# A routed expert kernel: the last expert's low parts on VectorE, each gather one job sooner

## The chip, the cores and the metric

The kernel runs on one core of a Trainium2 chip. The metric is the device time of one launch in microseconds. The core has TensorE (PE: matmuls and transposes), VectorE (DVE), ScalarE (ACT), GpSimd (POOL) and a queue on SyncE (SP) that only issues transfers. Each engine works through its own instructions in order; between engines there are only semaphores.

## The reference

For 4 x 512 tokens of 512 features, attention without values comes first, and then a mixture of experts:

```python
x = x + softmax(scores(ctx @ Wq.T + bq, ctx @ Wk.T + bk) * layernorm(x) + mask)   # (4, 512, 512)
t = layernorm(x)                                    # 2048 tokens x 512
shared = silu(t @ shared_gate_w) * (t @ shared_up_w) @ shared_down_w
logits = t @ router_w                               # 8 experts, the best 2 are taken
probs  = sigmoid(logits) at the two best, 0 elsewhere
gate, up = split(einsum('etd,edf->etf', probs.T[:, :, None] * t, gate_up_w))
out = x + shared + einsum('eti,eid->etd', silu(gate) * up, down_w).sum(axis=0)
```

## The kernel before

Work is cut into 55 jobs of 128 rows. Jobs 0 to 15 are the 16 tiles of tokens; each passes through the attention and then the shared expert, at place 0 of the weights. Jobs 16 to 54 are the 39 routed jobs: each has 128 rows of one expert. In between (about 121 to 145 us) DVE works out from the logits which token goes into which row of which job, and writes the tables jexpert (expert of a job), jgather and jscatter (rows to fetch and to add to), and jneed (see below). Experts follow one another in order, so that those of a low number come first; the trace shows four or five jobs for each.

Every product in the mixture is made of three: high by high, high by low and low by high. A tensor is split into a rounded high part and a low part, the difference of value and high part. For the weights this is done once. They come in 27 chunks (CHUNKS) of 128 x 1024 values, three to each expert: c // 3 is the place and c % 3 the third, two for gate_up and one for down. The SP queue loads a chunk into one of three stage buffers (L276), ScalarE makes the high part (high_part, L501, semaphore hi_s) and GpSimd the low part (low_part, L362, semaphore lo_s). SP's load of chunk c waits until chunk c-3 has its low part. Most chunks are done under the shared jobs. Chunks 22 to 24 get their low parts (late_low) after the first four gathers and 25 and 26 between the routed jobs, where ScalarE makes their high parts after jobs 17 and 18. The last chunks' places were used by other buffers until then (the four xn rows, for one), hence the waits in late_low.

A routed job n has these steps. GpSimd gathers its rows from the normalized tokens in memory into xg (gather, L423), four buffers deep. TensorE transposes them (x_transpose, L1133) while it works on job n-1; ScalarE makes x_hi and x_bf (L514, L515), DVE x_lo (L679). TensorE then makes the gate and up products (L963, L968, L1007), ScalarE the activation (L603), DVE the gating product h (gated, L878, semaphore h_s), the last to read xg. TensorE transposes h (L1016), its parts are made (L522, L523, and h_low at L685), and TensorE makes the down product (L1028, L1031, L1034) within job n+1. DVE copies it to y (y_routed, L887), four buffers deep, and GpSimd adds y to the output rows (scatter, L442) by an accumulating transfer.

In job n TensorE's order is: gate and up high of n, transpose of h of n-1, gate and up rest of n, transposes of n+1, down of n-1. DVE's order is: h_low(n-1), gated(n), x_low(n+1), y_routed(n-1).

Two rows of one token in jobs of different experts may not be added at the same time. So a scatter waits on GpSimd for the completion of the three scatters before it: always while n < 23 (named first in the code), and after that as jneed says, only where the expert differs. The buffers of y are given back by the same completions. All gathers and scatters stand in GpSimd's one queue, gather(n+4) and then scatter(n), as the loop at L458 to L463 writes them.

TensorE waits before each routed job for the low parts of its weights: for the first eight jobs up to the expert's own third chunk (jlow), after that for all of them.

Of the kernel before, what the change touches and what calls it, by code (L numbers as in the profile page):

```python
# [8 lines left out]
TILES = T // P  # L9
# [7 lines left out]
JOBS = TILES + ROUTED  # L17
# [6 lines left out]
XS = 4  # L24
# [7 lines left out]
NC = K * TILES  # L32
CAREFUL = 8
READY = EARLY + 1
FIRST = TILES - LAG
BIAS = 7


def build(nc, x, ctx, mask, kpad, wq, bq, wk, bk, router_w, gate_up_w, down_w, sg_w, su_w, sd_w, out):
# [10 lines left out]
    with stack:  # L50
        def sem(name):
            return stack.enter_context(nc.semaphore(name))
# [161 lines left out]
        st_trash, st_p8 = sem("st_trash"), sem("st_p8")  # L214

        c_ident, c_half, c_table, zero_s = sem("c_ident"), sem("c_half"), sem("c_table"), sem("zero_s")
        hi_s, lo_s, rwhi_s, rwlo_s = sem("hi_s"), sem("lo_s"), sem("rwhi_s"), sem("rwlo_s")
        bq_ready, wT_ps, wT_ready, ctxT_ps, ctxT_ready, proj_ps, proj_ready = (
            sem("bq_ready"), sem("wT_ps"), sem("wT_ready"), sem("ctxT_ps"), sem("ctxT_ready"), sem("proj_ps"),
            sem("proj_ready"))  # L220
# [88 lines left out]
        def _(pool):  # L309
# [63 lines left out]
                        zeros[:].unsqueeze(1).to_broadcast([P, XS, D])).then_inc(st_trash, 16)  # L373

            def late_low(c):
                place, i = c // 3, c % 3
                if i < 2:
                    t = TILES - XS + 2 * (place - 7) + i
                    pool.wait_ge(st_xn[t % XS], stored_xn(t))
                    pool.wait_ge(xT_ps, t + 1)  # L380
                else:
                    pool.wait_ge(max_s, TILES)
                low_part(c)
# [64 lines left out]
            pool.wait_ge(st_p8, 16)  # L448
            for n in range(TILES, TILES + XS):
                gather(n)  # L450
            for c in range(READY, READY + 3):
                late_low(c)
            for t in range(TILES - X2S, TILES):
                pool.wait_ge(st_y[t % X2S], stored_y(t))
            pool.wait_ge(st_trash, 16)
            pool.wait_ge(scatter_s, 1)
            pool.wait_ge(need_s, XS - 1)
            for n in range(TILES, JOBS):  # L458
                if n + XS < JOBS:
                    gather(n + XS)  # L460
                scatter(n)
                if n in (TILES + 1, TILES + 2):
                    late_low(READY + 3 + n - TILES - 1)  # L463
            for n in range(JOBS - XS, JOBS):
                pool.wait_ge(add_y[n % XS], 16 * ((n - TILES) // XS + 1))

# [154 lines left out]
        def _(dve):  # L621
# [74 lines left out]
            def y_shared(n):  # L696
                dve.wait_ge(y_ps, n + 1)
                dve.wait_ge(xn_s, n + 1)
                v.tensor_tensor(x2[:, n % X2S, :], ps_y(n)[:], x2[:, n % X2S, :], ALU.add).then_inc(y_s, 1)  # L699
# [136 lines left out]
            def tables():  # L836
# [4 lines left out]
                then(v.tensor_tensor(hole[:], hole[:], pidx[:, 0:ROUTED], ALU.mult))  # L841
                v.scalar_tensor_tensor(jscatter[:], tok[:], -1.0, hole[:], ALU.add, ALU.add).then_inc(scatter_s, 1)

            fetch(0, 0, FIRST)
            x_low(TILES - 2)
            last_normal()
# [21 lines left out]
            h_low(TILES - 2)  # L868
            scatter_waits()
            y_shared(FIRST - 1)  # L870
            h_low(TILES - 1)
            y_shared(TILES - 2)
            y_shared(TILES - 1)
# [16 lines left out]
            for n in range(TILES, JOBS):  # L890
                if n > TILES:
                    h_low(n - 1)
                gated(n)
                if n + 1 < JOBS:
                    x_low(n + 1)
                if n > TILES:
                    y_routed(n - 1)
# [4 lines left out]
        def _(pe):  # L902
# [236 lines left out]
            for n in range(TILES, JOBS):  # L1139
                e = pe.value_load(jexpert[0:1, n - TILES:n - TILES + 1], min_val=0, max_val=E)  # L1140
                if n < TILES + CAREFUL:
                    low = pe.value_load(jlow[0:1, n - TILES:n - TILES + 1], min_val=6, max_val=CHUNKS)
                    pe.wait_ge(lo_s, low)
                else:
                    pe.wait_ge(lo_s, CHUNKS)
                gate_up_high(n, e)
                if n > TILES:
                    h_transpose(n - 1)
                gate_up_low(n, e)
                gate_up_rest(n, e)  # L1150
                if n + 1 < JOBS:
                    x_transpose(n + 1)
                if n > TILES:
                    down(n - 1, before)
                before = e
# [24 lines left out]
```

## Time and profile before

| | us |
|---|---|
| median of 3 runs | 353.49 (353.42 to 355.19) |
| the profiled execution, its own time | 353.46 |
| its span, first to last instruction | 351.6 |
| TensorE busy | 318.0 (90%) |
| DVE busy | 206.8 (59%) |
| ScalarE busy | 181.0 (51%) |
| GpSimd busy | 212.2 (60%) |

The profile is of one execution. A span is counted from the first instruction to the last; the time of the execution has 1.86 us more around it. Job 16 begins on TensorE at 153.55 us and the last of its matmuls are at 343 us, so over half of the span is routed jobs.

### The profile page before, as it was taken

How to read it: one execution, taken by the hardware profiler on the slowest of the kernel's cores; microseconds unless marked ns; L12 is line 12 of the kernel's file. 1: busy time of each engine (PE TensorE's matmuls, PEld its weight loads, DVE VectorE, ACT ScalarE, POOL GpSimd, SP SyncE). 2: the span in 40 equal slices, each digit the busy share in tenths (PEclk: the TensorE clock that was granted, in tenths of full speed). 3: DMA queues.
4: the chain of work that ended last, by engine and by line, in shares of the span. 5: the costliest groups of instructions: out<-in, count | busy, mean ns of one | idle time of the engine just before them, and what ended most of it. 6: DMA issues, size and time to landing. Idle time of an engine off the chain costs nothing.

```text
span 351.6 us, 6597 instructions
## 1 busy us (share of the span) xinstructions
PE 318.0 (90%) x1677; PEld 222.4 (63%) x1677; DVE 206.8 (59%) x453; ACT 181.0 (51%) x409; POOL 212.2 (60%) x206
## 2 busy tenths in 40 slices
PE   2868999899999897879998989999999999999990
PEld 1334666676777666647766757777777777777760
DVE  0695888899998799834443444444444444445440
ACT  2578777767868745135544434444344444434430
POOL 0699999988686700393683666665465565555333
PEclk9989999999999999699999999999999999999998
DMA  7956678856755421281556486666666576565635
GB/s 175 320 216 230 213 239 241 245 204 209 236 159 187 170 92 7 66 292 38 90 97 115 70 170 99 109 110 118 117 122 108 88 128 108 115 123 100 113 45 75
DMA packets 29762, 50.60 MB, mean 144 GB/s; under 512 B 5472, under 2 KB 9312, under 8 KB 29728
## 3 DMA queue, kind: packets, MB, share of 16 engines
q0 software_dynamic: 9008, 21.66, 34.4%
q1 hardware_dynamic: 19232, 27.99, 24.7%
q10 hardware_dynamic: 1488, 0.54, 0.7%
q8 instruction: 16, 0.26, 0.3%
q14 instruction: 18, 0.15, 0.1%
HBM read 30.45 MB, written 19.73 MB: 143 GB/s over the span
## 4 chain that ended last, share of the span: by engine, by line
PE 60%; POOL 12%; DMA 10%; issue 9%; DVE 4%; SPq 2%; ACT 2%; POOLq 0%; DVEq 0%; ACTq 0%
PE bank L963 10%; PE bank L1007 10%; PE bank L968 8%; DMA out_rows<-y,jscatter 6%; PE bank L1028 4%; PE bank L1034 4%; PE bank L1031 4%; POOL gu_lo L362 4%; PE bank L1133 4%; PE bank L1016 2%; POOL dn_lo L362 2%; DMA xin<-in_x 2%; PE bank L926 2%; PE bank L985 2%; PE bank L935 2%
## 5 line engine op out<-in xcount | busy, mean ns | idle before, releaser
L442 POOL DMA_INDIRECT out_rows<-y,jscatter x39 | 61.9, 1587 | 74.1 <-DMA out_rows<-y,jscatter 52.1
L1007 PE MATMUL bank<-gu_hi,x_lo 128*128 (+1 forms) x220 | 72.8, 452 | 0.6 <-DVE x_lo L679 0.6
L963 PE MATMUL bank<-gu_hi,x_hi 128*128 (+1 forms) x220 | 61.6, 402 | 3.7 <-ACT x_hi L514 2.6
L423 POOL DMA_INDIRECT xg<-xn_rows,jgather x39 | 41.7, 1069 | 27.5 <-DVE jgather L839 15.3
L1007 PEld LDWEIGHTS bank<-gu_hi,x_lo 128*128 128x128 f32 x220 | 41.3, 189 | 18.0 <-issue 4.3
L878 DVE SCALAR_TENSOR_TENSOR h<-bank,xg,h 128x256 f32<-128x256 f32 x39 | 18.9, 484 | 56.0 <-ACT h L603 56.0
L522 ACT CAST h_hi<-bank 128x256 fp32r<-128x256 f32 x55 | 20.5, 374 | 60.7 <-PE bank L1016 57.0
L963 PEld LDWEIGHTS bank<-gu_hi,x_hi 128*128 128x128 f32 x220 | 40.0, 188 | 14.7 <-issue 2.8
L679 DVE TENSOR_TENSOR x_lo<-bank,x_hi 128x512 fp32r<-128x512 f32 x55 | 37.9, 690 | 19.0 <-ACT x_bf L515 18.6
L362 POOL TENSOR_TENSOR gu_lo<-stage,gu_hi 128x1024 bf16<-128x1024 f32 x18 | 43.4, 2410 | 5.6 <-ACT gu_hi L501 5.6
L603 ACT ACTIVATE h<-bank,xg 128x256 f32<-128x256 f32 x39 | 18.5, 474 | 50.0 <-PE bank L1007 26.4
L968 PE MATMUL bank<-gu_lo,x_bf 128*128 (+1 forms) x172 | 44.2, 379 | 0.0
L685 DVE TENSOR_TENSOR h_lo<-bank,h_hi 128x256 fp32r<-128x256 f32 x55 | 23.1, 420 | 32.9 <-ACT h_bf L523 32.8
L1034 PE MATMUL bank<-dn_hi,h_lo 128*128 (+1 forms) x86 | 35.5, 494 | 0.0
L514 ACT CAST x_hi<-bank 128x512 fp32r<-128x512 f32 x55 | 31.9, 581 | 6.3 <-PE bank L1133 4.3
L515 ACT CAST x_bf<-bank 128x512 bf16<-128x512 f32 x55 | 32.9, 598 | 0.0
L1028 PE MATMUL bank<-dn_hi,h_hi 128*128 (+1 forms) x86 | 30.8, 439 | 2.1 <-DVE x L699 1.0
L887 DVE COPY y<-bank 128x512 f32<-128x512 f32 x39 | 26.6, 681 | 1.3 <-PE bank L1034 1.3
L1031 PE MATMUL bank<-dn_lo,h_bf 128*128 (+1 forms) x86 | 26.5, 391 | 0.0
L1133 PE MATMUL bank<-ident,xg 128*128 128x128 f32 x156 | 23.5, 273 | 2.2 <-DMA xg<-xn_rows,jgather 2.2
L357 POOL TENSOR_TENSOR pen<-mask_pen,kpad_pen 128x512 bf16<-128x512 bf16 x16 | 18.6, 1160 | 10.1 <-DVE kpad_pen L705 10.0
L362 POOL TENSOR_TENSOR dn_lo<-stage,dn_hi 128x1024 bf16<-128x1024 f32 x9 | 21.9, 2438 | 4.5 <-ACT dn_hi L501 4.4
(145 smaller groups left out, 553.2 us busy)
## 6 DMA issues: line engine op xcount, KB each, us to landing
stage<-in_L_ffn_gate_up_w SPq DMA_DIRECT2D x16, 512.0 KB, 3.9
xin<-in_x SPq DMA_DIRECT2D x16, 256.0 KB, 4.4
xn_rows<-xn SPq DMA_DIRECT2D x16, 256.0 KB, 4.0
stage<-in_L_ffn_down_w SPq DMA_DIRECT2D x8, 512.0 KB, 3.7
out_rows<-x SPq DMA_DIRECT2D x16, 256.0 KB, 4.3
out_rows<-zeros POOLq DMA_DIRECT2D x1, 1024.0 KB, 5.0
ctx_in<-in_ctx SPq DMA_DIRECT2D x1, 768.0 KB, 8.8
xg<-xn_rows,jgather POOLq DMA_INDIRECT x39
```

Of the source, the lines that this page charges most:

```text
L362: g.tensor_tensor(third((gu_lo, dn_lo), c), stage[:, c % 3], third((gu_hi, dn_hi), c).bitcast(f32), ALU.subtract).then_inc(lo_s, 1)
L423: g.indirect_dma_start(out=xg[:, r, :], out_offset=None, in_=xn_dram, in_offset=bass.IndirectOffsetOnAxis(ap=jgather[:, n - TILES:n - TILE ...
L442: g.indirect_dma_start(out=out, out_offset=bass.IndirectOffsetOnAxis(ap=jscatter[:, n - TILES:n - TILES + 1], axis=0), in_=y[:, r, :], in_ ...
L515: a.copy(x_bf[:, n % TS], rows_T(n)).then_inc(xbf_s, 1)
L679: v.tensor_tensor(x_lo[:, n % TS], rows_T(n), x_hi[:, n % TS].bitcast(f32), ALU.subtract).then_inc(xlo_s, 1)
L963: tn.matmul(ps_g(n)[:], x_hi[:, n % TS, k, :], gu_hi[:, e, k, :], start=(k == 0), stop=False)
L968: tn.matmul(ps_g(n)[:], x_bf[:, n % TS, k, :], gu_lo[:, e, k, :], start=False, stop=False)
L1007: last = tn.matmul(ps_g(n)[:], x_lo[:, n % TS, k, :], gu_hi[:, e, k, :], start=False, stop=(k == KC - 1))
L1028: tn.matmul(ps_y(n)[:], h_hi[:, n % 2, c, :], dn_hi[:, e, c, :], start=(c == 0), stop=False)
L1031: tn.matmul(ps_y(n)[:], h_bf[:, n % 2, c, :], dn_lo[:, e, c, :], start=False, stop=False)
L1034: last = tn.matmul(ps_y(n)[:], h_lo[:, n % 2, c, :], dn_hi[:, e, c, :], start=False, stop=(c == IC - 1))
L1133: last = tn.transpose(ps_xT[n % 2][:, k * P:(k + 1) * P], xg[:, n % XS, k * P:(k + 1) * P], ident[:])
```

## The change

The low parts of chunks 24, 25 and 26 (the last expert, LAST = 24) are made by DVE instead of GpSimd, with a semaphore of their own, lolast_s. The first stands in DVE's order after the y of tile 13 and ahead of h_low(15); the other two in jobs 18 and 19 between h_low and the gating product. TensorE waits for lo_s up to 24 and, from job 24 on, for lolast_s too. GpSimd's loop issues gather(20) ahead of the loop and then gather(n+5) ahead of scatter(n), where it was gather(n+4). A gather's own wait (h_s of the job that held its buffer) is the same.

```diff
--- before.py
+++ after.py
@@ -32,6 +32,7 @@
 NC = K * TILES
 CAREFUL = 8
 READY = EARLY + 1
+LAST = CHUNKS - 3
 FIRST = TILES - LAG
 BIAS = 7
 
@@ -214,7 +215,7 @@
         st_trash, st_p8 = sem("st_trash"), sem("st_p8")
 
         c_ident, c_half, c_table, zero_s = sem("c_ident"), sem("c_half"), sem("c_table"), sem("zero_s")
-        hi_s, lo_s, rwhi_s, rwlo_s = sem("hi_s"), sem("lo_s"), sem("rwhi_s"), sem("rwlo_s")
+        hi_s, lo_s, lolast_s, rwhi_s, rwlo_s = sem("hi_s"), sem("lo_s"), sem("lolast_s"), sem("rwhi_s"), sem("rwlo_s")
         bq_ready, wT_ps, wT_ready, ctxT_ps, ctxT_ready, proj_ps, proj_ready = (
             sem("bq_ready"), sem("wT_ps"), sem("wT_ready"), sem("ctxT_ps"), sem("ctxT_ready"), sem("proj_ps"),
             sem("proj_ready"))
@@ -373,9 +374,8 @@
                         zeros[:].unsqueeze(1).to_broadcast([P, XS, D])).then_inc(st_trash, 16)
 
             def late_low(c):
-                place, i = c // 3, c % 3
-                if i < 2:
-                    t = TILES - XS + 2 * (place - 7) + i
+                if c % 3 < 2:
+                    t = TILES - XS + c % 3
                     pool.wait_ge(st_xn[t % XS], stored_xn(t))
                     pool.wait_ge(xT_ps, t + 1)
                 else:
@@ -448,19 +448,18 @@
             pool.wait_ge(st_p8, 16)
             for n in range(TILES, TILES + XS):
                 gather(n)
-            for c in range(READY, READY + 3):
+            for c in range(READY, LAST):
                 late_low(c)
             for t in range(TILES - X2S, TILES):
                 pool.wait_ge(st_y[t % X2S], stored_y(t))
             pool.wait_ge(st_trash, 16)
             pool.wait_ge(scatter_s, 1)
             pool.wait_ge(need_s, XS - 1)
+            gather(TILES + XS)
             for n in range(TILES, JOBS):
-                if n + XS < JOBS:
-                    gather(n + XS)
+                if n + XS + 1 < JOBS:
+                    gather(n + XS + 1)
                 scatter(n)
-                if n in (TILES + 1, TILES + 2):
-                    late_low(READY + 3 + n - TILES - 1)
             for n in range(JOBS - XS, JOBS):
                 pool.wait_ge(add_y[n % XS], 16 * ((n - TILES) // XS + 1))
 
@@ -841,6 +840,17 @@
                 then(v.tensor_tensor(hole[:], hole[:], pidx[:, 0:ROUTED], ALU.mult))
                 v.scalar_tensor_tensor(jscatter[:], tok[:], -1.0, hole[:], ALU.add, ALU.add).then_inc(scatter_s, 1)
 
+            def last_low(c):
+                if c % 3 < 2:
+                    t = TILES - 2 + c % 3
+                    dve.wait_ge(st_xn[t % XS], stored_xn(t))
+                    dve.wait_ge(xT_ps, t + 1)
+                else:
+                    dve.wait_ge(max_s, TILES)
+                dve.wait_ge(hi_s, c + 1)
+                v.tensor_tensor(third((gu_lo, dn_lo), c), stage[:, c % 3], third((gu_hi, dn_hi), c).bitcast(f32),
+                                ALU.subtract).then_inc(lolast_s, 1)
+
             fetch(0, 0, FIRST)
             x_low(TILES - 2)
             last_normal()
@@ -868,6 +878,7 @@
             h_low(TILES - 2)
             scatter_waits()
             y_shared(FIRST - 1)
+            last_low(LAST)
             h_low(TILES - 1)
             y_shared(TILES - 2)
             y_shared(TILES - 1)
@@ -890,6 +901,8 @@
             for n in range(TILES, JOBS):
                 if n > TILES:
                     h_low(n - 1)
+                if n in (TILES + 2, TILES + 3):
+                    last_low(LAST + n - TILES - 1)
                 gated(n)
                 if n + 1 < JOBS:
                     x_low(n + 1)
@@ -1139,10 +1152,11 @@
             for n in range(TILES, JOBS):
                 e = pe.value_load(jexpert[0:1, n - TILES:n - TILES + 1], min_val=0, max_val=E)
                 if n < TILES + CAREFUL:
-                    low = pe.value_load(jlow[0:1, n - TILES:n - TILES + 1], min_val=6, max_val=CHUNKS)
+                    low = pe.value_load(jlow[0:1, n - TILES:n - TILES + 1], min_val=6, max_val=LAST)
                     pe.wait_ge(lo_s, low)
                 else:
-                    pe.wait_ge(lo_s, CHUNKS)
+                    pe.wait_ge(lo_s, LAST)
+                    pe.wait_ge(lolast_s, CHUNKS - LAST)
                 gate_up_high(n, e)
                 if n > TILES:
                     h_transpose(n - 1)
```

## Rows read from the trace of the kernel before

**Rows 1.** Windows view: us, busy us (x instructions) of each engine, granted clock, DMA share, GB/s.

```profile
182.00:209.00 27.00, 24.68 (x123) 17.02 (x122) 11.24 (x21) 10.63 (x25) 15.94 (x12) 1.00 0.65 113
209.00:336.00 127.00, 127.00 (x644) 90.97 (x643) 58.47 (x108) 55.60 (x135) 69.59 (x52) 1.00 0.63 111
```

**Rows 2.** Timeline of TensorE: start us, us, engine, line, operation, idle before and its releaser.

```profile
157.86 1.19 PE L963 MATMUL bank<-gu_hi,x_hi 128*128 x4 [0.87 <-POOL gu_lo L362]
...
162.70 1.09 PE L963 MATMUL bank<-gu_hi,x_hi 128*128 x4
...
165.64 0.60 PE L1133 MATMUL bank<-ident,xg 128*128 128x128 f32 x4
...
168.38 0.38 PE L1016 MATMUL bank<-ident,h 128*128 128x128 f32 x2
...
181.70 1.09 PE L963 MATMUL bank<-gu_hi,x_hi 128*128 x4
...
185.65 0.66 PE L1133 MATMUL bank<-ident,xg 128*128 128x128 f32 x4 [0.85 <-DMA xg<-xn_rows,jgather]
...
187.85 1.20 PE L963 MATMUL bank<-gu_hi,x_hi 128*128 x4 [0.16 <-issue]
...
206.60 0.66 PE L1133 MATMUL bank<-ident,xg 128*128 128x128 f32 x4 [1.30 <-DMA xg<-xn_rows,jgather]
...
208.47 1.09 PE L963 MATMUL bank<-gu_hi,x_hi 128*128 x4
```

**Rows 3.** Chain that ended last, in order of time: start us, us, what.

```profile
164.82 4.86 DMA out_rows<-y,jscatter
...
201.07 5.49 DMA xg<-xn_rows,jgather
```

**Rows 4.** Timeline of GpSimd: low parts (L362), gathers (L423), scatters (L442).

```profile
146.71 1.03 POOL L423 DMA_INDIRECT xg<-xn_rows,jgather  x1 [0.30 <-issue]
...
150.41 2.39 POOL L362 TENSOR_TENSOR gu_lo<-stage,gu_hi 128x1024 bf16<-128x1024 f32 x1
...
155.08 2.36 POOL L362 TENSOR_TENSOR gu_lo<-stage,gu_hi 128x1024 bf16<-128x1024 f32 x1
158.68 1.03 POOL L423 DMA_INDIRECT xg<-xn_rows,jgather  x1 [1.24 <-DVE h L878]
164.82 1.64 POOL L442 DMA_INDIRECT out_rows<-y,jscatter  x1 [5.10 <-DVE y L887]
...
171.65 2.91 POOL L362 TENSOR_TENSOR gu_lo<-stage,gu_hi 128x1024 bf16<-128x1024 f32 x1
...
180.50 1.08 POOL L423 DMA_INDIRECT xg<-xn_rows,jgather  x1 [0.16 <-issue]
...
199.18 1.59 POOL L442 DMA_INDIRECT out_rows<-y,jscatter  x1 [2.69 <-DVE y L887]
201.07 1.07 POOL L423 DMA_INDIRECT xg<-xn_rows,jgather  x1 [0.30 <-issue]
```

**Rows 5.** Timeline of VectorE around the places of its new steps.

```profile
147.15 0.19 DVE L832 TENSOR_TENSOR other<-efl 128x38 f32<-128x38 f32 x1
...
150.78 0.42 DVE L685 TENSOR_TENSOR h_lo<-bank,h_hi 128x256 fp32r<-128x256 f32 x1 [1.90 <-ACT h_bf L523]
...
161.82 0.48 DVE L878 SCALAR_TENSOR_TENSOR h<-bank,xg,h 128x256 f32<-128x256 f32 x1 [1.42 <-ACT h L603]
...
166.55 0.49 DVE L878 SCALAR_TENSOR_TENSOR h<-bank,xg,h 128x256 f32<-128x256 f32 x1 [1.41 <-ACT h L603]
...
171.30 0.48 DVE L878 SCALAR_TENSOR_TENSOR h<-bank,xg,h 128x256 f32<-128x256 f32 x1 [1.40 <-ACT h L603]
```

**Rows 6.** Timeline of ScalarE: x_hi of job 17, high part of chunk 25.

```profile
157.07 0.58 ACT L514 CAST x_hi<-bank 128x512 fp32r<-128x512 f32 x1
...
162.50 1.08 ACT L501 CAST gu_hi<-stage 128x1024 fp32r<-128x1024 f32 x1
```

**Rows 7.** Groups by line on VectorE: busy us in all, mean ns of one.

```profile
L820 DVE TENSOR_TENSOR OB<-iotap,rowf 128x1024 bf16<-128x1024 bf16 x4 | 4.6, 1218 | 0.0
```

## The prediction

> **What bounds the kernel now.** I read the windows view first. In 209 to 336 us TensorE is busy 127.00 of 127.00 us, but in 182 to 209 us only 24.68 of 27.00, at a granted clock of 1.00 in both (2.4 GHz) [rows 1]. So the routed stage is TensorE's own pace with a hole in one place. In TensorE's timeline each job begins with one line L963 group. Job 18 begins at 162.70 and job 22 at 181.70: 19.00 us for 4 jobs, a pitch of 4.75. Job 27 begins at 208.47, so jobs 18 to 27 take 45.77 where nine pitches are 42.75: 3.02 us are lost. The rows show where: job 22 to job 23 takes 6.15 (1.40 too much) and in it the transposes for job 23 wait for "DMA xg" until 185.65; the transposes for job 27 wait for the same until 206.60 [rows 2]. What ends these waits is a late gather. The chain has the second one: 5.49 us of DMA from the gather issued at 201.07 [rows 3].
>
> Why is a gather late? In GpSimd's timeline gather(23) is issued at 180.50 and gather(27) at 201.07 [rows 4]. GpSimd's order is gather(n+4), scatter(n), and a scatter stands on its engine until the scatter before it has landed (the first seven always do, L440). Scatter(16) is issued at 164.82, scatter(22) at 199.18: a turn of 34.36 / 6 = 5.73 us against TensorE's 4.75 [rows 4]. So the gathers, each shut in behind a scatter, slip by about 1 us a job until the scatters after the seventh, which wait only where the expert changes, make it good. Two low parts of 2.9 us in the same queue (the one at 171.65 and its like a job later [rows 4]) make the early ones later still.
>
> **Part 1: each gather a job sooner.** Gather(n+5) now stands ahead of scatter(n). Its own wait is h_s of job n+1, whose gating product is the last reader of its buffer; DVE makes that product before y of job n, which the scatter behind it needs anyway. So nothing queued behind it (the scatter and all after) waits longer for data; what the queue adds is the gather's own 1.07 us. Gather(20) waits for h of job 16 and goes at 158.68, as now. Gather(21) needs h of job 17, at 161.82 + 0.48 = 162.30 [rows 5]; with the 0.86 that gather(20) took from its h (157.82 to 158.68 [rows 4, 5]) it is issued at 163.16 and is over at 164.25, before scatter(16) at 164.82. Gather(22): 167.04 + 0.86 = 167.9. Gather(23): 171.78 + 0.86, or behind scatter(17), some 172.6 instead of 180.50; it lands within 5.5 us, at about 178, and is wanted at 181.70 + 2.94 = 184.6 (2.94 is job 18's begin at 162.70 to its transposes at 165.64, the step of every job [rows 2]). Its stall of 1.40 goes. From then on gather(n+5) has the place in time that gather(n+4) had: gather(28) goes at 201.07, lands at 206.56, and is wanted, with no stall before, at 162.70 + 9 x 4.75 + 2.94 = 208.39. It makes it by 1.8 us. So the 1.52 us at job 27 go too (the last 0.10 lies at job 24, behind the first). Sum of this part: -3.02 us. Behind gather(28) the scatters catch up (3.26 us a turn: 1.59 + 0.30 + 1.07 + 0.30 [rows 4]), and leads grow.
>
> The scatters themselves keep their times: scatter(n) waits for scatter(n-1), and there is one gather between two scatters as before. Their chain must also not hold y: y of job n+4 overwrites the buffer of scatter(n). Scatter(22) lands by about 204.1 (199.18 and the 4.86 of scatter(16) [rows 3]), y(26) is due at 213.77 - 3.0 = 210.7. Cover of 6 us. At the end the last scatter follows y of job 54, which moves with TensorE.
>
> **Part 2: low parts of the last expert on DVE.** GpSimd loses three steps: chunk 24 at 155.08 (2.36) and chunks 25 and 26. TensorE waits for all chunks from job 24 on, at 192 us or later; chunk 25 is over at 171.65 + 2.91 = 174.56 now and chunk 26 a job later, so none is near its deadline. The profile names chunk 24 as the releaser of job 17's first matmul (157.86), but x_hi of that job ends at 157.07 + 0.58 = 157.65, after chunk 24's end at 157.44 [rows 2, 4, 6]: nothing is won there. The room in GpSimd's queue is worth nothing by itself beyond part 1, as gather(20) is held by h.
>
> DVE gains three tensor_tensor of 1024 elements with both inputs in SBUF. The trace has none so long in fp32; nearest are L820 with 1024 bf16 elements, 1.22 us, and GpSimd's own 2.36 as the other end [rows 4, 7]. I take 1.22, same engine and count. The first stands between the y of tile 13 and h_low of tile 15 (150.78), in 1.90 of idle time that begins at 148.88: 0.68 left. The second and third stand before the gating products of jobs 18 and 19, where DVE is idle 1.41 and 1.40 us waiting for the activation [rows 5]: 0.19 left. Their inputs are there: high part 25 is made at 162.50 to 163.58 [rows 6], the DVE step runs at 165.2. Cost 0. At 2.36 us the first would hold h_low by 0.46, and the start of the routed stage with it; the others would end 0.95 past the idle, and the transposes of h at 168.38 have 168.38 - 167.04 = 1.34 us of slack [rows 2, 5]. So 0 to +0.5. The SP queue is not touched: it waits for chunks up to 23 only, made by GpSimd at the same times.
>
> **Part 3: one more semaphore wait on TensorE's queue** in each of 31 jobs. Jobs 18 to 22 carry a register load more than the late jobs and their pitch is 4.75, as TensorE busy throughout shows for the late ones. No wait is exposed; 0, at most 31 x 0.01 = 0.3, an estimate, as a larger gap would show in the busy share of [rows 1].
>
> **A rule weighed.** The trace has DVE steps with two SBUF inputs inside a gather's issue: L832 at 147.15 takes 0.19 while GpSimd works on a gather from 146.71 to 147.74 [rows 4, 5]; it is not held. The Trainium skill ("SBUF — State Buffer", section "SBUF: two separate sides") says that a DVE step with two SBUF inputs and a GpSimd step that reads SBUF take one shared pair of ports in turn, the later one fully blocked. By that rule the first new step could be shut out. The row speaks against it for gathers; for the plain low part that starts at 150.41 no row does, but the new step should end by 150.3.
>
> **The rivals.**
> A, as worked out: 351.6 - 3.02 = 348.6 of span; the profiled execution's own time is 353.46, 1.86 more than its span, and 0.03 under the median 353.49. So 350.4 + 0.03: 350.5. Chance 0.76.
> B, only the first stall goes, or a smaller one stays: the turn of scatter grows a little because gathers now start nearer to scatters. Gather(28) goes 6 turns + 1.90 after 164.82 and needs 5.49: 172.21 + 6p must be under 208.39, so p under 6.03; it is 5.73. At 6.2, 1.0 us of stall stays, at 6.28 all of 1.5: 351.5 to 352.0. For it: the margin is 0.30 a turn. Against: order and number between scatters are unchanged. Chance 0.09.
> C, the first DVE step is shut out by GpSimd. Behind gather(19), which ends just before the low part begins at 150.41, it would end at 151.6 and h_low be 0.8 late; behind that low part (150.41 + 2.39 [rows 4]) it would end at 154.0, h_low 3.2 late. TensorE's start of the routed stage moves by as much: 350.5 + 0.8 to 3.2, 351.3 to 353.7. Against it: L832 ran freely. Chance 0.08. This is the time that the skill's rule would give.
> D, it ends slower: a gather's descriptors ahead of a scatter's in the one queue lengthen each scatter's landing by a gather's work, 1.07 to 1.37 us with its gap. Then p = 6.80 to 7.10, gather(28) is late by 172.21 + 6p - 208.39 = 4.6 to 6.4, less the 3.0: 355.1 to 356.9. It decides from p = 6.53. Against it: today a gather is issued right behind each scatter and the turn of 5.73 already holds it. Chance 0.04.
> E, nothing changes: the stalls have another cause than the gather's issue, and both stay: 353.5. Against it: transposes wait for that DMA by name and for nothing else. Chance 0.03.
>
> **How the numbers follow.** Predicted 350.5. The range reaches below to 349.9 (an uncertainty of 0.5 us, of pitches read to a few hundredths and of the spread of runs) and above to 352.2, over B and the smaller half of C. About 0.5% (1.8 us, so 351.7) is what a measurement of this kernel can tell from no change. Faster by more: A, half of B, a third of C, 0.83; within: 0.13; slower: 0.04.
>
> **What would show it.** The transposes of jobs 23 and 27 start with no idle, TensorE is busy throughout 158 to 206; gather(23) issued near 172.6 and the gather at about 201 is the 28th; scatter(22) at 199 +- 0.5; three DVE steps of 1.2 us in gaps, with h_low of tile 15 still at about 150.8 and job 18 at 162.7. It is wrong if a new idle with "DMA xg" appears at job 27 or 28 (B, D), or if job 16 starts after 153.6 (C).

## The result, and the profile after

The changed kernel took 351.49 us (median of 6 runs, 350.94 to 354.36), beside 354.55 for the kernel before in the runs taken with it. The ratio is 0.9923, with a 95% interval of 0.9895 to 0.9950: some 2.7 us faster. Two further sets of timed runs, each on a chip of its own, gave 0.9923 (0.9897 to 0.9948) and 0.9951 (0.9926 to 0.9976). The forecast of 350.5 against 353.5 is a ratio of 0.9915, inside the first two intervals and just below the third.

The profiled execution is the slowest of the six, 354.36 us with a span of 352.6, which is 1.0 longer than the span of before. So the sum can't be read off the spans, and the stages must be compared one by one. Windows of the changed kernel (the columns are those of [rows 1]: TensorE, its weight loads, VectorE, ScalarE, GpSimd, then the granted clock, the DMA share and GB/s):

```profile
20.00:40.00 20.00, 15.69 (x65) 8.65 (x63) 12.20 (x29) 14.79 (x27) 17.30 (x15) 0.83 0.55 176
120.00:140.00 20.00, 18.25 (x120) 13.20 (x119) 15.20 (x54) 9.29 (x20) 5.08 (x8) 0.91 0.34 96
158.00:182.00 24.00, 23.09 (x115) 16.53 (x116) 12.26 (x21) 12.01 (x26) 10.38 (x8) 1.00 0.52 125
182.00:209.00 27.00, 27.00 (x139) 19.26 (x138) 12.08 (x23) 11.69 (x29) 13.88 (x11) 1.00 0.54 91
209.00:336.00 127.00, 127.00 (x643) 91.35 (x643) 59.36 (x108) 55.73 (x134) 72.00 (x55) 1.00 0.67 116
```

The last two rows answer to [rows 1]. The hole is gone: in 182 to 209 us TensorE is busy 27.00 of 27.00, where it was 24.68. The 0.9 of idle in 158 to 182 is the second routed job's wait for its first x_hi, which lies in that window here since all came later. The kernel before has the same wait at 157.86 [rows 2].

TensorE's timeline (start us, us, then the group of instructions; line L976 answers to L963 of before, L1146 to L1133):

```profile
158.05 1.20 PE L976 MATMUL bank<-gu_hi,x_hi 128*128 x4 [0.83 <-ACT x_hi L513]
...
162.35 1.19 PE L976 MATMUL bank<-gu_hi,x_hi 128*128 x4 [0.87 <-issue]
...
167.18 1.09 PE L976 MATMUL bank<-gu_hi,x_hi 128*128 x4
...
189.12 0.60 PE L1146 MATMUL bank<-ident,xg 128*128 128x128 f32 x4
...
209.91 1.09 PE L976 MATMUL bank<-gu_hi,x_hi 128*128 x4
...
212.84 0.60 PE L1146 MATMUL bank<-ident,xg 128*128 128x128 f32 x4
```

Job 16 begins at 158.05, job 18 at 167.18 and job 27 at 209.91: 42.73 us for nine jobs, where [rows 2] have 45.77. The transposes for job 23 (189.12) and for job 28 (212.84) show no idle time before them, where those for jobs 23 and 27 waited for "DMA xg". But job 16 begins 4.5 us later than the 153.55 of the kernel before, and that is all that makes the span longer: its span has 194.55 us from there to the end, before it was 198.05.

GpSimd's timeline of the same kernel, for [rows 4]:

```profile
153.84 1.53 POOL L423 DMA_INDIRECT xg<-xn_rows,jgather  x1 [0.30 <-issue]
...
163.18 1.03 POOL L423 DMA_INDIRECT xg<-xn_rows,jgather  x1 [3.06 <-DVE h L889]
167.56 1.01 POOL L423 DMA_INDIRECT xg<-xn_rows,jgather  x1 [3.35 <-DVE h L889]
169.31 1.64 POOL L442 DMA_INDIRECT out_rows<-y,jscatter  x1 [0.73 <-issue]
...
175.11 1.89 POOL L442 DMA_INDIRECT out_rows<-y,jscatter  x1 [1.69 <-DMA out_rows<-y,jscatter]
177.30 1.08 POOL L423 DMA_INDIRECT xg<-xn_rows,jgather  x1 [0.30 <-issue]
...
204.59 1.61 POOL L442 DMA_INDIRECT out_rows<-y,jscatter  x1 [2.74 <-issue]
206.50 1.07 POOL L423 DMA_INDIRECT xg<-xn_rows,jgather  x1 [0.30 <-issue]
```

The order is as forecast. Gather(20) at 163.18 waits for h, gather(21) at 167.56 is now ahead of scatter(16) at 169.31, gather(23) is issued at 177.30, 19.25 us after job 16's begin (before: 180.50 - 153.55 = 26.95), and the gather behind scatter(22) (204.59) is number 28, at 206.50, 48.45 us after job 16's begin (201.07 - 153.55 = 47.52 by the prediction). The scatters have a turn of (204.59 - 169.31) / 6 = 5.88 us. Two steps are longer than before: the fourth gather takes 1.53 us instead of 1.01, and scatter(17) 1.89 instead of 1.59. Both start while one of VectorE's new steps runs (rows below).

VectorE's timeline around its three new steps (L851), for [rows 5]:

```profile
153.27 1.21 DVE L851 TENSOR_TENSOR gu_lo<-stage,gu_hi 128x1024 bf16<-128x1024 f32 x1
155.10 0.43 DVE L684 TENSOR_TENSOR h_lo<-bank,h_hi 128x256 fp32r<-128x256 f32 x1 [0.62 <-ACT h_bf L522]
...
169.54 1.22 DVE L851 TENSOR_TENSOR gu_lo<-stage,gu_hi 128x1024 bf16<-128x1024 f32 x1
171.04 0.48 DVE L889 SCALAR_TENSOR_TENSOR h<-bank,xg,h 128x256 f32<-128x256 f32 x1 [0.28 <-ACT h L602]
...
174.30 1.22 DVE L851 TENSOR_TENSOR dn_lo<-stage,dn_hi 128x1024 bf16<-128x1024 f32 x1
```

A step is 1.21 or 1.22 us. Behind the first, 0.62 us are left of the idle time ahead of h_low; behind the second the gating product starts with 0.28 left.

### The profile page after: what moved, and what is told of

Read it like the earlier page. It is cut to its first block, busy times and chain, and to the rows that moved or that the text cites. A ratio compares the mean times of both kernels' runs of the same rounds, so it can differ in the third digit from the quotient of the medians.

```text
span 352.6 us, 6628 instructions
## 1 busy us (share of the span) xinstructions
PE 320.0 (91%) x1677; PEld 224.4 (64%) x1677; DVE 211.2 (60%) x456; ACT 181.1 (51%) x409; POOL 206.1 (58%) x203
## 4 chain that ended last, share of the span: by engine, by line
PE 74%; POOL 10%; issue 5%; DVE 4%; ACT 2%; DMA 2%; ACTq 0%; DVEq 0%; POOLq 0%
PE bank L976 13%; PE bank L1020 13%; PE bank L981 10%; PE bank L1041 6%; PE bank L1047 6%; PE bank L1044 6%; PE bank L1146 5%; PE bank L1029 3%; POOL gu_lo L363 3%; POOL pen L358 2%; PE bank L939 2%; PE bank L998 2%; DMA kpad_in<-in_mask_BxS_bf 2%; POOL dn_lo L363 2%; PE bank L948 2%
## 5 line engine op out<-in xcount | busy, mean ns | idle before, releaser
L442 POOL DMA_INDIRECT out_rows<-y,jscatter x39 | 62.3, 1596 | 69.8 <-DMA out_rows<-y,jscatter 35.9
L976 PE MATMUL bank<-gu_hi,x_hi 128*128 (+1 forms) x220 | 63.1, 409 | 3.6 <-ACT x_hi L513 2.7
L423 POOL DMA_INDIRECT xg<-xn_rows,jgather x39 | 42.2, 1083 | 36.3 <-DVE jgather L838 16.8
L976 PEld LDWEIGHTS bank<-gu_hi,x_hi 128*128 128x128 f32 x220 | 41.1, 193 | 14.5 <-ACT x_hi L513 2.6
L363 POOL TENSOR_TENSOR gu_lo<-stage,gu_hi 128x1024 bf16<-128x1024 f32 x16 | 38.1, 2382 | 8.3 <-ACT gu_hi L500 8.2
L981 PEld LDWEIGHTS bank<-gu_lo,x_bf 128*128 128x128 bf16 x172 | 16.5, 98 | 11.9 <-issue 1.6
L1029 PE MATMUL bank<-ident,h 128*128 128x128 f32 x110 | 22.1, 283 | 1.5 <-DVE h L692 1.5
```

Source lines behind the costliest of these rows:

```text
L363: g.tensor_tensor(third((gu_lo, dn_lo), c), stage[:, c % 3], third((gu_hi, dn_hi), c).bitcast(f32), ALU.subtract).then_inc(lo_s, 1)
L423: g.indirect_dma_start(out=xg[:, r, :], out_offset=None, in_=xn_dram, in_offset=bass.IndirectOffsetOnAxis(ap=jgather[:, n - TILES:n - TILE ...
L442: g.indirect_dma_start(out=out, out_offset=bass.IndirectOffsetOnAxis(ap=jscatter[:, n - TILES:n - TILES + 1], axis=0), in_=y[:, r, :], in_ ...
L976: tn.matmul(ps_g(n)[:], x_hi[:, n % TS, k, :], gu_hi[:, e, k, :], start=(k == 0), stop=False)
L981: tn.matmul(ps_g(n)[:], x_bf[:, n % TS, k, :], gu_lo[:, e, k, :], start=False, stop=False)
L1029: last = tn.transpose(ps_hT[:, c * P:(c + 1) * P], h[:, n % 2, c * P:(c + 1) * P], ident[:])
```

## The experiments

### The same two kernels again

> The changed kernel once more, for a second profile: its first one began the routed stage 4.5 us later than the kernel before did (158.05 against 153.55 us), although its routed stage was 3.3 us shorter. Theory (the late start belongs to that one execution): job 16 begins within 1 us of 153.6 and the span is about 348.5 to 350. Rival (the change makes the stages ahead of job 16 longer, by its code or its first DVE step): job 16 begins at 156 us or later again. Ratio to the kernel before, both theories from the timed runs: 0.992.

> The kernel before once more, for a second profile of it: both theories expect the waits for xg at jobs 23 and 27 of 1.4 and 1.5 us in sum again. It shows how much the begin of job 16 (153.55 us in the first profile) moves between executions of one kernel: within 0.5 us if the later begin of the changed kernel is its own, by 1 us or more if it is chance.

The changed kernel's job 16 began at 153.92 this time and its span was 348.7; the kernel before began it at 155.41, span 352.7. TensorE's timeline of the changed kernel, second profile:

```profile
153.92 1.18 PE L976 MATMUL bank<-gu_hi,x_hi 128*128 x4 [0.83 <-ACT x_hi L513]
...
163.05 1.09 PE L976 MATMUL bank<-gu_hi,x_hi 128*128 x4
```

And of the kernel before, second profile:

```profile
155.41 1.18 PE L963 MATMUL bank<-gu_hi,x_hi 128*128 x4 [1.08 <-ACT x_hi L514]
...
187.54 0.66 PE L1133 MATMUL bank<-ident,xg 128*128 128x128 f32 x4 [0.90 <-DMA xg<-xn_rows,jgather]
...
207.69 0.66 PE L1133 MATMUL bank<-ident,xg 128*128 128x128 f32 x4 [0.51 <-DMA xg<-xn_rows,jgather]
```

In the kernel before both waits for xg stand where they were, together 2.27 us instead of 3.02 (its jobs 22 to 23, 23 to 24 and 26 to 27 took 6.20, 4.85 and 5.47 us). From job 18's begin to job 54's it takes 173.98 and 173.24 us in its two profiles; the changed kernel takes 170.70, 171.16 and 171.14 in its three (the third is of the run below). The means differ by 2.6 us, which is what the timed runs say.

The late begin of job 16 differs from execution to execution, and no part of it could be tied to the change. It was 153.55 and 155.41 in one kernel and 158.05, 153.92 and 155.37 in the other; two kernels below that have no new step on VectorE ahead of job 16 began it at 156.03 and 156.22. In the first profile of the changed kernel the granted clock was 0.83 in 20 to 40 us and 0.91 in 120 to 140 (the windows above); in the first of the kernel before it was 0.91 and 1.00. GpSimd's first low part began at 18.71 us in the kernel before and at 20.28 in the changed one. All of this lies ahead of anything that the change touches.

### Each part alone

Gathers a job sooner, low parts left on GpSimd:

```diff
+            gather(TILES + XS)
             for n in range(TILES, JOBS):
-                if n + XS < JOBS:
-                    gather(n + XS)
+                if n + XS + 1 < JOBS:
+                    gather(n + XS + 1)
                 scatter(n)
```

> Only the gathers are a job sooner; GpSimd keeps all low parts. Theory (the late gathers are the whole loss): no transposes wait for xg, all 3.0 us are gained and the time is that of the full change within 0.3 us. Its GpSimd queue: low part 25 behind scatter(17), gather(23) behind it at about 174.7 us, wanted at 184.6, so still in time; low part 26 behind scatter(18), gather(24) at 180.5, wanted at 189.4. Rival (the freed queue of GpSimd is needed too): one wait for xg of 1 to 1.5 us stays, or the span is over 1 us longer than with both parts.

Low parts on VectorE as in the change, with the old loop of gather(n + XS) and scatter(n):

> Only the low parts move to DVE; gathers stay as in the kernel before. Theory: gather(23) goes right behind scatter(18), at about 178.2 instead of 180.5 us, lands by 183.7 and is in time, so the wait at job 23 goes; but gather(27) is behind scatter(21), whose turn is set by the landing of the scatters, still at about 201, and is now wanted 1.4 us earlier: its wait grows from 1.5 to about 2.9. Sum 0, within 0.3 us of the kernel before. Rival (low parts in the queue cost what they take): 1.4 us or more are gained.

Gathers alone: ratio 0.9928 (0.9901 to 0.9955), on the chip where the whole change gave 0.9923. Job 18 to job 54 takes 170.95 us, and there is no wait for xg. GpSimd's timeline of that kernel:

```profile
152.50 1.01 POOL L423 DMA_INDIRECT xg<-xn_rows,jgather  x1 [0.30 <-issue]
...
174.34 2.93 POOL L362 TENSOR_TENSOR gu_lo<-stage,gu_hi 128x1024 bf16<-128x1024 f32 x1
177.43 1.08 POOL L423 DMA_INDIRECT xg<-xn_rows,jgather  x1 [0.16 <-DMA out_rows<-y,jscatter]
...
180.24 2.88 POOL L362 TENSOR_TENSOR dn_lo<-stage,dn_hi 128x1024 bf16<-128x1024 f32 x1
183.28 1.08 POOL L423 DMA_INDIRECT xg<-xn_rows,jgather  x1 [0.16 <-issue]
```

The low part of chunk 25 (174.34) still holds gather(23) back to 177.43, and that of chunk 26 (180.24) gather(24) to 183.28, and neither matters. The freed queue was not needed. The fourth gather takes 1.01 us here.

Low parts alone: 0.9992 (0.9968 to 1.0016), nothing. TensorE's groups that waited for xg in that kernel:

```profile
197.97 0.66 PE L1145 MATMUL bank<-ident,xg 128*128 128x128 f32 x4 [0.15 <-DMA xg<-xn_rows,jgather]
...
204.03 0.66 PE L1145 MATMUL bank<-ident,xg 128*128 128x128 f32 x4 [1.08 <-DMA xg<-xn_rows,jgather]
...
209.76 0.66 PE L1145 MATMUL bank<-ident,xg 128*128 128x128 f32 x4 [0.77 <-DMA xg<-xn_rows,jgather]
```

The wait for job 23 is gone, as expected, and the gain is lost again: jobs 25, 26 and 27 begin 0.37, 1.30 and 0.98 us late, 2.65 in all. I had expected one wait of 2.9 at job 27. The size is right, but it is spread over three gathers, each late by itself, as the scatters fall behind a little in every turn. The gain of the change is its first part, and the second is worth nothing that can be measured.

### The turn of the scatters, longer and shorter

If the first seven scatters, each waiting for the one before, are what makes gathers late, then a longer turn must bring the waits back in the changed kernel, by 6 us for each us of a turn. A memset on GpSimd was put between the landing of a scatter and the issue of the next (512 elements, and 1024 in the second kernel):

```diff
                         pool.wait_ge(add_y[(n - d) % XS], 16 * ((n - d - TILES) // XS + 1))
+                if first and n > TILES:
+                    then(g.memset(ballast[:, 0:512], 0.0))
                 g.indirect_dma_start(
```

> The changed kernel with a GpSimd memset of 512 elements (0.53 us at L370 of the kernel before, about 0.6 with its wait) between the landing of each scatter and the issue of the next, in the six turns from scatter(16) to scatter(22). Theory (the turn of the scatters decides whether gathers are in time, with a margin of about 1.5 us over six turns in the second profile of the changed kernel: gather(28) issued 201.79, landing at about 207.3, wanted at 208.7): six turns of 0.6 are 3.6 us, so about 2.1 us of waits for xg come back, by job 27. Rival (gathers have ample lead, and the turn has slack to give): no wait for xg, time as the changed kernel's.

> The same with a memset of 1024 elements, about 1.05 us a turn. Theory: 6.3 us over six turns, less the margin of 1.5: 4.8 us of waits for xg, so that the kernel is 1.8 us slower than the one before the change. Each extra us of a turn costs 6 us from the threshold on (2.7 us more than the run with 512 elements). Rival: under 1 us of waits.

GpSimd's timeline of the kernel with 512 elements:

```profile
166.84 1.64 POOL L445 DMA_INDIRECT out_rows<-y,jscatter  x1 [0.73 <-issue]
...
171.79 0.53 POOL L444 MEMSET ballast<- 128x512 f32 x1 [0.85 <-DMA out_rows<-y,jscatter]
173.21 1.61 POOL L445 DMA_INDIRECT out_rows<-y,jscatter  x1 [0.90 <-POOL ballast L444]
...
205.57 1.61 POOL L445 DMA_INDIRECT out_rows<-y,jscatter  x1 [0.91 <-POOL ballast L444]
```

Its turn is (205.57 - 166.84) / 6 = 6.46 us; with 1024 elements it was 6.81. With 512, one wait came back, job 27 to job 28 taking 6.18 us, 1.43 too much; ratio 1.0000 (0.9975 to 1.0024). With 1024, job 26 to job 27 took 6.17 and job 27 to job 28 6.79, together 3.46 too much; ratio 1.0057 (1.0032 to 1.0081). TensorE's timeline there:

```profile
205.72 0.66 PE L1149 MATMUL bank<-ident,xg 128*128 128x128 f32 x4 [1.20 <-DMA xg<-xn_rows,jgather]
...
212.51 0.66 PE L1149 MATMUL bank<-ident,xg 128*128 128x128 f32 x4 [1.83 <-DMA xg<-xn_rows,jgather]
```

The two sizes differ by 2.03 us for 6 x 0.35 = 2.1 us of turn: the slope is the six turns. Both waits are less than I had written (2.1 and 4.8), and both give the same point from which a wait comes: 6.46 - 1.43/6 = 6.22 and 6.81 - 3.46/6 = 6.23 us a turn, not the 6.03 of the prediction. The term that was mis-sized is the landing of a gather. I took the 5.49 of [rows 3] for all of them. Gather(28) was issued at 207.49 in the kernel with 512 elements and its rows were being transposed at 211.77, 4.3 us later (4.2 with 1024 elements: 208.31 to 212.51), and in the second profile of the kernel before gather(27) took 4.7 (202.99 to 207.69). The 1.2 us less are 0.2 a turn. So the point of 6.22 holds for a gather that lands in 4.3 us, and one that takes longer brings the wait sooner (see the first of the two versions further down).

The other way round, the turn was made short in the kernel before, and nothing else: its first seven scatters wait only where the expert changes, as the later ones do.

```diff
-                first = n < TILES + 2 * XS - 1
-                need = [] if first else [needed(n, d) for d in range(1, XS)]
+                need = {d: needed(n, d) for d in range(1, XS) if n - d >= TILES}
                 pool.wait_ge(y_s, n + 1)
-                for d in range(1, XS):
-                    if not first:
-                        pool.wait_ge(add_y[(n - d) % XS], need[d - 1])
-                    elif n - d >= TILES:
-                        pool.wait_ge(add_y[(n - d) % XS], 16 * ((n - d - TILES) // XS + 1))
+                for d in need:
+                    pool.wait_ge(add_y[(n - d) % XS], need[d])
+                if n < TILES + XS:
+                    pool.wait_ge(add_y[n % XS], 16)
...
+            for i in range(XS):
+                g.dma_start(first_turn[i], ident[:, 0:E]).then_inc(add_y[i], 16)
             pool.wait_ge(pexp_s, TILES)
```

(The four small transfers take 2.4 us of GpSimd's idle time ahead of the routed stage; jneed and the other waits on these semaphores are 16 higher.)

> The kernel before, with gathers and low parts as they are there, but its first seven scatters wait by the expert too, as the later ones do (four small transfers, issued while GpSimd is idle ahead of the routed stage, start the four semaphores so that every wait is for a positive number). Theory (the turn of 5.7 us of the first seven scatters, which wait for each other's landing without need, is what makes gathers late): scatters 17 to 20 go as their y is ready, every 4.75 us, no transposes wait for xg, and the old order of gathers gains the same 3.0 us: ratio about 0.992. Rival (the order of the queue is the cause, whatever the turn): a wait of 1 us or more stays.

Ratio 0.9925 (0.9901 to 0.9950), no wait for xg, job 18 to job 54 in 170.95 us: the whole gain, with gathers and low parts as they were. GpSimd's scatters in that kernel:

```profile
167.54 1.66 POOL L444 DMA_INDIRECT out_rows<-y,jscatter  x1 [5.17 <-DVE y L889]
...
172.20 1.58 POOL L444 DMA_INDIRECT out_rows<-y,jscatter  x1 [1.61 <-DVE y L889]
...
177.77 1.59 POOL L444 DMA_INDIRECT out_rows<-y,jscatter  x1 [0.30 <-issue]
...
183.32 1.58 POOL L444 DMA_INDIRECT out_rows<-y,jscatter  x1 [0.31 <-issue]
...
186.58 1.59 POOL L444 DMA_INDIRECT out_rows<-y,jscatter  x1 [0.30 <-issue]
```

They come after 4.66, 5.57, 5.55 and 3.26 us; the middle two are held by the low parts of chunks 25 and 26 on the same queue, not by a landing. So one cause is shown from three sides: longer turns bring the waits, shorter ones take them away, and issuing gathers a job sooner avoids them.

### The first step on VectorE, twice

The low part of chunk 24 is made twice, one step behind the other; twice_low is the same step once more, with a semaphore of its own.

```diff
+            twice_low(LAST)
             last_low(LAST)
             h_low(TILES - 1)
```

> The changed kernel with the first of DVE's new steps (chunk 24) made twice, one behind the other. Theory of the cover: one step of 1.21 us leaves 0.62 us of idle ahead of h_low of tile 15, so the second makes h_low about 0.6 us late, and TensorE waits for it as long; the other two steps stay hidden. Theory of the shared ports (the second to start is held): gather(19) takes 1.53 us again, as it starts while the first DVE step runs, and GpSimd's low part 22 behind it, which now starts while the second DVE step runs, is longer than 2.38 us by up to what is left of that step (0.3 to 0.6); the DVE steps stay at 1.21 us. Rival (no sharing, the 1.53 is of the fourth gather itself): low part 22 stays at 2.38.

> The changed kernel a third time, on the chip of the next run, to be compared with it: ratio 0.992; job 18 to job 54 takes 171.0 us within 0.3; gather(19) takes 1.53 us and scatter(17) 1.9 us once more, where the kernel before has 1.01 and 1.59.

> The run low_twice once more, as its timed runs were 0.6% slower than the changed kernel's on another chip, while its profile shows no wait for the second step. Theory (the cover of 0.6 us is gone only in executions in which TensorE does the shared down products at the full clock, so the cost is between 0 and 0.6 us): ratio to the changed kernel of this chip 1.000 to 1.002. Rival (a step of 1.2 us there costs 2 us by a way that I have not seen): 1.005 or more again.

The timed runs of the first set gave 0.9984 (0.9962 to 1.0006) on one chip, those of the second 0.9959 (0.9936 to 0.9982), where the changed kernel had 0.9951 (0.9926 to 0.9976) beside it (0.992 had been expected there). That is 1.001 by this pair, with an uncertainty of some 0.0035: room for anything from 1 us less to 1.5 us more. What the second step costs on average is not shown by the times. In the first profile TensorE did not wait at all. In the second it did, TensorE's timeline:

```profile
154.94 0.73 PE L1058 MATMUL bank<-dn_hi,h_lo 128*128 128x512 f32 x2 [1.14 <-DVE h_lo L685]
...
157.00 2.07 PE L987 MATMUL bank<-gu_hi,x_hi 128*128 x4 [0.89 <-POOL gu_lo L364]
158.87 1.73 PE L992 MATMUL bank<-gu_lo,x_bf 128*128 x4
```

The second step makes h_low late, and TensorE waits 1.14 us for it, twice what I had expected; the usual wait ahead of job 16 follows, 0.89 us here. Then the granted clock falls. Windows view of the same profile:

```profile
157.00:161.00 4.00, 4.00 (x11) 2.35 (x12) 0.69 (x1) 0.22 (x1) 2.10 (x1) 0.59 0.84 240
```

The granted clock is 0.59 there (it was 0.99 in 150 to 157 us); taken by single microseconds it is 0.50 from 157 to 160, which is the lower level, 1.2 GHz. The four matmuls that begin at 157.00 take 2.07 us where the same group takes 1.18 in the changed kernel, and job 16 lasts 5.82 us instead of 4.30. With the wait itself that is 2.6 us in this execution. That the wait brought the fall is likely but was seen once: the kernel before, in its second profile, had 0.46 and then 1.08 us of waits ahead of job 16 and kept a granted clock of 1.00. Whether TensorE waits at all depends on the execution, by these two profiles: where the down products just ahead run at the lower clock, as in the first profile (granted clock 0.72 in 148 to 154 us, down of tile 14 from 150.11 to 152.83; in the second 1.00, and 150.33 to 151.78), h is ready later and hides the step. My estimate of 0 to 0.6 was wrong at its upper end.

It also shows how thin the change's own cover is: in the third profile of the changed kernel h_low started without idle time behind the single step, at 152.71, and the matmul that needs it began 0.49 us after the one ahead of it, where the second profile of the kernel before has 0.25. That is 0.2 us.

The rule of the shared ports. GpSimd's timeline in the second profile of the kernel with the step made twice:

```profile
154.21 2.57 POOL L364 TENSOR_TENSOR gu_lo<-stage,gu_hi 128x1024 bf16<-128x1024 f32 x1
156.74 2.37 POOL L364 TENSOR_TENSOR dn_lo<-stage,dn_hi 128x1024 bf16<-128x1024 f32 x1
```

The low part that starts at 154.21, while VectorE's second step runs (153.33 to 154.56), takes 2.57 us, and 2.58 in the first profile; the next one, with no such step beside it, 2.37. The fourth gather took 1.52 to 1.55 us in every kernel with the step and 1.01 or 1.02 in the four profiles of kernels without it (both of the kernel before, gathers alone, and the kernel before with the short turn). Scatter(17) gives the counter-check. It took 1.81 to 1.98 us wherever it began while VectorE's third new step ran. In the two kernels with a memset the step was over when scatter(17) began (171.84 + 1.22 = 173.06 against 173.21 us with 512 elements), and it took 1.61. A memset of 1024 elements that began together with a step, at 170.55 us, took 0.95, no longer than the others like it: of the GpSimd steps seen beside one, only this one, which reads nothing, was not held.

### Two versions that go further

Job 17 waits 0.87 us for its x_hi in every version so far. Its transposes, x_hi and x_low were moved ahead of job 16's products, into the wait of job 16, and the transpose of job 16's h was put one group later:

```diff
             x_transpose(TILES)
+            x_transpose(TILES + 1)
...
                 gate_up_high(n, e)
-                if n > TILES:
+                if n > TILES + 1:
                     h_transpose(n - 1)
                 gate_up_low(n, e)
+                if n == TILES + 1:
+                    h_transpose(n - 1)
                 gate_up_rest(n, e)
-                if n + 1 < JOBS:
+                if TILES < n < JOBS - 1:
                     x_transpose(n + 1)
```

> The changed kernel, with the second routed job's transposes, x_hi and x_low made ahead of the first job's gate and up products, and the first job's h transposed a little later. Job 16 and job 17 each wait 0.8 to 0.9 us on TensorE for x_hi (158.05 and 162.35 us in the first profile of the changed kernel). Theory: job 17's wait goes, and its transposes are made in the wait of job 16, so from job 16's begin to job 18's it is 7.7 us instead of 9.13: 1.4 us gained, ratio to the kernel before about 0.988. Rival: the later h of job 16 holds the down product of job 17's time, and under 0.7 us are gained.

Ratio 0.9898 (0.9872 to 0.9923). TensorE's timeline:

```profile
155.61 1.20 PE L978 MATMUL bank<-gu_hi,x_hi 128*128 x4 [1.04 <-ACT x_hi L513]
...
158.46 1.08 PE L978 MATMUL bank<-gu_hi,x_hi 128*128 x4
...
163.38 1.19 PE L978 MATMUL bank<-gu_hi,x_hi 128*128 x4
```

From job 16 to job 18 it is 7.77 us instead of 9.13, as expected. But further on 0.93 us came back: jobs 27 and 28 begin 0.83 and 0.10 late, the first with a wait for xg. GpSimd's timeline of that kernel, scatters 18 and 19 and gather(27):

```profile
178.02 1.57 POOL L442 DMA_INDIRECT out_rows<-y,jscatter  x1 [3.34 <-DVE h L890]
...
185.35 1.59 POOL L442 DMA_INDIRECT out_rows<-y,jscatter  x1 [4.38 <-issue]
...
199.00 1.06 POOL L423 DMA_INDIRECT xg<-xn_rows,jgather  x1 [0.31 <-issue]
```

I took this for jobs that run 1.4 us sooner while the scatters do not, as the expectation below says. The rows speak against that: scatter(16) began 165.35 - 155.61 = 9.74 us after job 16, where the changed kernel has 11.26, so the chain began sooner by as much as the jobs. It then lost time on its way: one turn took 185.35 - 178.02 = 7.33 us and the mean of six was 6.27, and gather(27), issued at 199.00, was used at 205.16, 6.2 us later, where 4.1 to 5.5 are seen for the late gathers of the other kernels. So landings were slow in this profile, and the margin could not take it. Why they were slow is open, and with one profile it isn't shown that the new order causes it. With the short turn of the scatters added:

> The run fill, with these scatter waits too. In fill 0.9 us of waits for xg came back at jobs 27 and 28, as jobs run 1.4 us sooner there and the scatters do not. Theory: with scatters of one expert free they go, and the time is 0.9 us under that of fill and about 1.4 us under the changed kernel's: ratio to the kernel before about 0.988. Rival: the three register loads that each early scatter gets hold GpSimd, and nothing is gained over fill.

The waits for xg are gone (job 18 to job 54 in 171.04 us, 172.16 in the version before it) and the span of the profiled execution was 348.8, against 350.6 of the changed kernel on the same chip. The timed ratio is 0.9913 (0.9885 to 0.9942), where the changed kernel had 0.9951 beside it: 0.4% under it, with intervals that overlap. Against that version, timed on another chip, nothing is shown. The stage tells the gain, the total can't, for its spread of 1 to 1.5 us either way from execution to execution is larger.

## Why the prediction was right, and where it was not

**The bound and the hole.** Right. The two waits for xg were the loss, and they went. The removed 3.02 us of the sum were those of one profile; a second one of the same kernel has 2.27, as gather(27) landed 0.8 us sooner there (5.5 and 4.7 us). By the means of all profiles of the two kernels the routed stage gains 2.6 us, and the ratios of the timed runs say 1.7 to 2.7. So the sum took the loss of one execution for that of all.

**The times of the gathers.** Right in order and nearly in time: gather(23) 19.25 us after job 16's begin (19.1 by the prediction), gather(28) in the place of gather(27), 0.9 us later than forecast. The scatters' turn is 5.79 to 5.90 in the changed kernel's three profiles and 5.73 and 5.74 in the two of the kernel before. "The scatters themselves keep their times" was off by 0.1 us a turn, which is the 0.9 us. Where it comes from is not settled: the turn was 5.83 with the gathers alone, but 5.86 with the low parts alone, where the gathers stand in their old places. The 0.2 to 0.4 us by which scatter(17) is longer beside VectorE's step are at most 0.06 of a turn. So rival D's mechanism is not shown, and if it acts, it is at a tenth of its price.

**The margin of 1.8 us** at gather(28) came out at about that, by two errors that nearly cancel. The landing was taken too long (5.49 us, where 4.2 and 4.3 were measured behind the longer turns), which moves the point from 6.03 to 6.22 us a turn, and the turn was taken too short (5.73, where 5.79 to 5.90 were measured): 6.22 less 5.79 to 5.90, six times, is 1.9 to 2.6 us. That the sizes cancel is luck; a landing of 6.2 us, as in the first version that goes further, would have used most of it.

**The low parts on VectorE.** The step cost 1.22 us as taken. 0.62 and 0.71 us of idle time were left behind it in two profiles (0.68 forecast); in the third none, and 0.2 us showed. Part 2 was rightly given no gain.

**The rule of the ports.** The prediction doubted it because a small step ran freely inside a gather's issue. That row shows one order only. In the other order, where a gather, a scatter or a low part of GpSimd begins while VectorE's step of 1.2 us with two SBUF inputs runs, the GpSimd step was longer in every profile that has the case, by 0.52, 0.30 and 0.2 us in those read here, each a little less than what was left of the step (0.64, 0.41 and 0.35). So this half of the rule of the Trainium skill ("SBUF — State Buffer", section "SBUF: two separate sides") agrees with the traces. The half by which VectorE would be held does not agree, as far as issues go: its step took 1.22 us at 169.54 with scatter(16)'s issue under way since 169.31, and 1.21 at 153.27 inside the gather of 152.52 to 153.53. No run put a new step behind a plain low part of GpSimd, the costlier case of rival C: the low part began after it in all of them. Rival C did not come.

**The wait on TensorE's queue** cost nothing that can be seen. From job 27's begin to job 54's, where every job has it, the changed kernel takes 127.97, 128.38 and 128.43 us in its three profiles and the kernel before 128.21 and 128.22.

**The total.** 350.5 was forecast, 351.49 measured. The median of the kernel before, from which the forecast starts, was 353.49 over three runs and is 354.55 over the six beside the change; that alone is the 1.0 us. The difference of the medians is 3.06 us, next to the 3.02 of the sum, but that closeness is luck: the interval of the ratio leaves 1.8 to 3.7 us, and the stage, read in several profiles, gained 2.6. The term that was a little too large is the loss of 3.02 us.

## What to carry to other kernels

When a transfer is late, look at what its queue does before it, and whether those waits are needed at all: here the first seven scatters waited for each other's landing where only a change of expert asks for it. A chain that turns slower than the consumer is no cost until its lag has eaten the lead of what is queued within it; work out the turn at which that happens, and measure it by making the turn longer. And to read a gain smaller than the spread, compare a stage from its own begin in several profiles, not spans.

## What the runs showed of the hardware

A VectorE step of 1.2 us with two SBUF inputs holds back a GpSimd tensor_tensor, or the issue of an indirect transfer, that begins while it runs: the gather's 1.01 us became 1.52 to 1.55, in all ten profiles that have the case. A step of VectorE that began during such an issue was not longer (1.21 to 1.23 us). From issue to use, late gathers took 4.1 to 6.2 us. Waits of 1.14 and 0.89 us on TensorE were followed in one execution by a granted clock of 0.59 over the next 4 us, and job 16 took 1.5 us more; waits of 0.46 and 1.08 us at the same place in another did not bring it. The begin of the routed stage moved by 4.5 us between executions with no change of the code ahead of it that matters, along with the granted clock in 20 to 40 us (0.76 to 0.91 over all profiles) and the begin of GpSimd's first low part (18.7 to 20.3 us).
